# Splitting the epilogue's layer norm in two: statistics of a tile issued ahead of the next tile's preparation

## The chip, the cores and the metric

The kernel runs on the 8 cores of one Trainium2 chip (two dies of four cores). Each core computes 2048 of the 16384 rows. The metric is the device time of the slowest core in microseconds; lower is better.

## What is computed

A "sandwich" layer on x of 16384 x 1024, in fp32 at its borders. The reference, cut to its core:

```python
def _L0_attn_ref(x, Wq, bq, Wk, bk, Wv, bv):
    q = einsum('bte,de->btd', x, Wq) + bq
    k = einsum('bte,de->btd', x, Wk) + bk
    v = einsum('bte,de->btd', x, Wv) + bv
    p = softmax(einsum('bqd,bkd->bqk', q, k) / 32)
    return einsum('bqk,bkd->bqd', p, v)

def _L0_ffn_ref(x, W1, b1, W2, b2):      # BitNet: ternary weights, 8-bit activations
    h = gelu(bitlinear(x, W1, b1))
    return bitlinear(h, W2, b2)

x = x + _layernorm(_L0_attn_ref(_layernorm(x), ...))
x = x + _layernorm(_L0_ffn_ref(_layernorm(x), ...))
```

## The kernel before, in words

The whole program is written down through a small planner (`Plan`). `pl.op` and `pl.group` append instructions to one list for each engine, in the order in which the Python code calls them, and put waits in front of an instruction for the buffers that it reads and writes. Nothing reorders anything later: the order of calls is the order on each engine. A buffer is tracked as a whole (`bt(name)`), so the second of two transfers into the same buffer waits for the first.

There are four stages.

1. Layer norm of all 16384 rows into a DRAM scratch, quantising of the two FFN weights into DRAM scratches, and the q projection (0 to about 985 us in the profile).
2. Attention: 16 groups of 1024 keys by 4 groups of 512 queries, unnormalised z summed in `z_acc` in SBUF (to about 2976 us). Then the row sums' reciprocals go through DRAM into `linv_col` (to about 3040 us).
3. The epilogue of attention, which the change touches: 16 tiles of 128 rows, numbered t.
4. The FFN, again 16 tiles, after its weights have been loaded (3260 us to the end).

For a tile t the epilogue has three helpers, all with double buffers chosen by t % 2 but for the single `ep_znbf`:

- `ep_zn(t)`: VectorE scales `z_acc` by `linv_col` into `ep_znbf` (L817, called "zn" below); TensorE transposes it in 8 pieces into `ps_tz` (L825); VectorE copies the result to `ep_znfm` (L832, "the copy").
- `ep_proj(t)`: TensorE multiplies `ep_znfm` by `wv_ep`, 16 matmuls of 512 columns (L844) and 2 for the bias (L850), into `ps_pj`. I call these 18 matmuls the burst of tile t.
- `ep_out(t)`: the layer norm of `ps_pj` by `emit_ln` (two `bn_stats` L539 and L542, `bn_aggr` L545, plus-epsilon L548, all VectorE; the square root L551 on ScalarE; reciprocal L554 and the shift L557 on VectorE), then VectorE scales `ps_pj` into `x2_stage` (L868) and adds the residual `xr_tile` (L873). ScalarE issues the load of the residual two tiles ahead (L808), GpSimd issues the store of `x2_stage` (L880).

The loop (L885 to L894) calls `ep_zn(0)`, `ep_proj(0)`, and then for each t: `ep_zn(t+1)`, `ep_proj(t+1)`, `ep_out(t)`. So VectorE's list in one round is zn(t+1), copy(t+1), the whole of out(t). When the last projection, tile 15, has been emitted, the counts of all semaphores are kept in `gate_pj`.

After the epilogue SyncE's queue loads the FFN weights. The 32 transfers into `w2q_sb` (L906) are in order, each waiting for the one before. Transfers 0 to 15 wait only for the end of attention; transfer 16 waits for `gate_pj`, since its place in SBUF overlaps `wv_ep`. Behind the 16 last ones stand 8 transfers into `w1q_sb` (L916) and then the first loads of `x2_tile` (L935), which the FFN's first instruction (`emit_ln` in `stage_x(0)`) reads.

Of the kernel before, what the change touches and what calls it, by code (L numbers as in the profile page):

```python
# [10 lines left out]
AF = mybir.ActivationFunctionType  # L11
ALU = mybir.AluOpType
# [20 lines left out]
EPS = 1e-5  # L33
# [132 lines left out]
def build_program():  # L166
# [28 lines left out]
    pl = Plan()  # L195
    B = {}

    def bt(name):
        if name not in B:
            B[name] = BufT()  # L200
        return B[name]

    with ExitStack() as ctx:
# [64 lines left out]
        ln_scr2 = [at(f"ln_scr2_{i}", [P, 16], F32) for i in range(2)]  # L268
# [33 lines left out]
        def ms(ap_, val):  # L302
# [4 lines left out]
            out=ident[:], in_=ident[:], compare_op=ALU.not_equal, fill=1.0,  # L307
            base=0, pattern=[[-1, P]], channel_multiplier=1),
            reads=[bt("ident")], writes=[bt("ident")])
# [7 lines left out]
        for ec in range(EC):  # L317
            pl.op("gpsimd", lambda eng, ec=ec: eng.dma_start(
                out=bq_col[:, ec:ec + 1],
                in_=bq_in[ec * P:(ec + 1) * P].rearrange("(p o) -> p o", o=1)),  # L320
                writes=[bt("bq_col")], dma="LD_G")
        pl.op("gpsimd", lambda eng: eng.dma_start(
            out=bv_bcast[0:1, :], in_=bv_in[:]),
            writes=[bt("bv_bcast")], dma="LD_G")
        for (src, dst, nm) in ((wkt, wkt_sb, "wkt_sb"),
                               (wqt, wqt_sb, "wqt_sb")):
            for ec in range(EC):
                pl.op("gpsimd", lambda eng, s=src, d=dst, ec=ec:
                      eng.dma_start(out=d[:, ec, :],
                                    in_=s[ec * P:(ec + 1) * P, :]),  # L330
                      writes=[bt(nm)], dma="LD_G")
# [7 lines left out]
        def m_name(e_):  # L339
            return f"k_stage{e_}" if e_ < 4 else f"v_stage{e_ - 4}"  # L340

        for half in range(2):
# [7 lines left out]
                reads=[bt("bq_col"), bt("wkt_sb")], writes=[bt("ps_k0")])  # L350
        pl.op("vector", lambda eng: eng.tensor_copy(
            out=bq_row[0:1, :], in_=ps_k[0][0:1, :]),
            reads=[bt("ps_k0")], writes=[bt("bq_row")])
        for ec in range(EC):
# [3 lines left out]
            for half in range(2):  # L358
                for sc in range(EC):
# [8 lines left out]
                     reads=[bt("wqt_sb"), bt("wkt_sb")], writes=[psb])  # L368
            pl.op("scalar", lambda eng, ec=ec, pp=pp: eng.copy(
                out=m_chunks[ec][:], in_=ps_k[pp][:]),  # L370
                reads=[psb], writes=[bt(m_name(ec))])
# [166 lines left out]
        def emit_ln(eng_scr, scr_b, src_ap, src_b):  # L538
            pl.op("vector", lambda eng: eng.bn_stats(  # L539
                out=eng_scr[:, 0:6], in_=src_ap[:, 0:512]),  # L540
                reads=[src_b], writes=[scr_b])
            pl.op("vector", lambda eng: eng.bn_stats(  # L542
                out=eng_scr[:, 6:12], in_=src_ap[:, 512:1024]),
                reads=[src_b], writes=[scr_b])
            pl.op("vector", lambda eng: eng.bn_aggr(  # L545
                out=eng_scr[:, 12:14], in_=eng_scr[:, 0:12]),
                reads=[scr_b], writes=[scr_b])
            pl.op("vector", lambda eng: eng.tensor_scalar_add(  # L548
                out=eng_scr[:, 14:15], in0=eng_scr[:, 13:14], scalar1=EPS),
                reads=[scr_b], writes=[scr_b])  # L550
            pl.op("scalar", lambda eng: eng.activation(  # L551
                out=eng_scr[:, 14:15], in_=eng_scr[:, 14:15], func=AF.Sqrt),
                reads=[scr_b], writes=[scr_b])
            pl.op("vector", lambda eng: eng.reciprocal(  # L554
                out=eng_scr[:, 14:15], in_=eng_scr[:, 14:15]),
                reads=[scr_b], writes=[scr_b])
            pl.op("vector", lambda eng: eng.scalar_tensor_tensor(  # L557
                out=eng_scr[:, 15:16], in0=eng_scr[:, 12:13], scalar=-1.0,
                in1=eng_scr[:, 14:15], op0=ALU.mult, op1=ALU.mult),
                reads=[scr_b], writes=[scr_b])  # L560
# [65 lines left out]
        for g in range(NT_OWN // 4):  # L626
            xp = g % 4
            xfm = bt(f"xn_fm{xp}")
            for dc in range(DC):
# [7 lines left out]
                    for e_ in range(EC)]  # L637
# [6 lines left out]
                         reads=[bt(m_name(e_)) for e_ in range(EC)] +  # L644
                               [xfm, bt("bq_row"), bt("ones_row5")],
                         writes=[psb])
                pl.op("scalar", lambda eng, dc=dc, g=g:
                      eng.copy(  # L648
                          out=q_fm[:, dc, g * 512:(g + 1) * 512],
                          in_=ps_k[0][:, 0:512]),  # L650
                      reads=[psb], writes=[bt("q_fm")])
# [38 lines left out]
        for kg in range(NKG):  # L690
            par = kg % 2
            kb, vb = bt(f"k_buf{par}"), bt(f"v_buf{par}")
            if kg == NKG - 1:
                wv_gate = list(dict(pl.cnt).items())
                for ec in range(EC):
                    pl.op("gpsimd", lambda eng, ec=ec: eng.dma_start(
                        out=wv_ep[:, ec, :], in_=wvt[ec * P:(ec + 1) * P, :]),
                        writes=[bt("wv_ep")], dma="LD_G", extra=wv_gate)
            for qg in range(NQG):
                for kt in range(KT_PG):  # L700
# [9 lines left out]
                        reads=[kb, bt("q_fm")], writes=[pss])  # L710
                    pl.op("scalar", lambda eng, kt=kt, sp=sp: eng.activation(  # L711
                        out=p_sb[:, kt, :], in_=ps_s[sp][:], func=AF.Exp,
                        scale=1.0 / 32.0, bias=c_nshift[:]),
                        reads=[pss, bt("c_nshift")], writes=[bt("p_sb")])
                for qt in range(4):
# [8 lines left out]
                        reads=[bt("p_sb"), vb], writes=[psz])  # L724
# [5 lines left out]
                    reads=[bt("p_sb"), bt("ones_col")], writes=[bt("ps_l")])  # L730
                for qt in range(4):
                    psz = bt(f"ps_z{qt}")
                    t_own = qg * 4 + qt
                    if kg == 0:
                        pl.op("vector", lambda eng, qt=qt, t=t_own:
                              eng.tensor_copy(out=z_acc[:, t, 0:512],
                                              in_=ps_z[qt][:]),
                              reads=[psz], writes=[bt(f"z_acc{t_own}")])
                    else:
                        pl.op("vector", lambda eng, qt=qt, t=t_own:  # L740
                              eng.tensor_add(out=z_acc[:, t, 0:512],  # L741
                                             in0=ps_z[qt][:],
                                             in1=z_acc[:, t, 0:512]),
                              reads=[psz, bt(f"z_acc{t_own}")],
                              writes=[bt(f"z_acc{t_own}")])
                if kg == 0:
                    pl.op("vector", lambda eng, qg=qg: eng.tensor_copy(
                        out=l_acc[0:1, qg * QG:(qg + 1) * QG], in_=ps_l[:]),
                        reads=[bt("ps_l")], writes=[bt(f"l_acc{qg}")])
                else:  # L750
                    pl.op("vector", lambda eng, qg=qg: eng.tensor_add(
                        out=l_acc[0:1, qg * QG:(qg + 1) * QG], in0=ps_l[:],
                        in1=l_acc[0:1, qg * QG:(qg + 1) * QG]),
                        reads=[bt("ps_l"), bt(f"l_acc{qg}")],
                        writes=[bt(f"l_acc{qg}")])
                for qt in range(4):
# [9 lines left out]
                        reads=[bt("p_sb"), vb], writes=[psz])  # L766
                for qt in range(4):
                    psz = bt(f"ps_z{qt}")
                    t_own = qg * 4 + qt
                    if kg == 0:  # L770
                        pl.op("vector", lambda eng, qt=qt, t=t_own:
                              eng.tensor_copy(out=z_acc[:, t, 512:1024],
                                              in_=ps_z[qt][:]),
                              reads=[psz], writes=[bt(f"z_acc{t_own}")])
                    else:
                        pl.op("vector", lambda eng, qt=qt, t=t_own:
                              eng.tensor_add(out=z_acc[:, t, 512:1024],  # L777
                                             in0=ps_z[qt][:],
                                             in1=z_acc[:, t, 512:1024]),
                              reads=[psz, bt(f"z_acc{t_own}")],  # L780
                              writes=[bt(f"z_acc{t_own}")])
            if kg + 2 < NKG:
# [6 lines left out]
              reads=la, writes=la)  # L789
        pl.op("gpsimd", lambda eng: eng.dma_start(  # L790
            out=l_scr.rearrange("(o q) -> o q", o=1), in_=l_acc[0:1, :]),
            reads=la, writes=[bt("l_scr")], dma="LD_G")
        for tt in range(NT_OWN):
            pl.op("gpsimd", lambda eng, tt=tt: eng.dma_start(
                out=linv_col[:, tt:tt + 1], in_=l_scr[tt * P:(tt + 1) * P]),
                reads=[bt("l_scr")], writes=[bt("linv_col")], dma="LD_G")
# [5 lines left out]
        ps_pj = [ps2e.enter_context(nc.psum_tensor(f"ps_pj{i}", [P, E], F32))  # L802
                 for i in range(2)]
# [34 lines left out]
        def ep_proj(t):  # L838
            par = t % 2
            builds = []  # L840
            for half in range(2):
                for e_ in range(EC):
# [15 lines left out]
                     writes=[bt(f"ps_pj{par}")],  # L858
                     extra=(att_gateE if t < 2 else ()))

        def ep_out(t):
            par = t % 2
            ls = ln_scr2[t % 2]
            lsb = bt(f"ln_scr2_{t % 2}")
            emit_ln(ls, lsb, ps_pj[par], bt(f"ps_pj{par}"))
            sp = t % 2
            pl.op("vector", lambda eng, ls=ls, sp=sp, par=par:
                  eng.tensor_scalar(  # L868
                      out=x2_stage[sp][:], in0=ps_pj[par][:],
                      scalar1=ls[:, 14:15], scalar2=ls[:, 15:16],  # L870
                      op0=ALU.mult, op1=ALU.add),
                  reads=[bt(f"ps_pj{par}"), lsb], writes=[bt(f"x2_stage{sp}")])
            pl.op("vector", lambda eng, par=par, sp=sp: eng.tensor_add(  # L873
                out=x2_stage[sp][:], in0=x2_stage[sp][:],
                in1=xr_tile[par][:]),
                reads=[bt(f"x2_stage{sp}"), bt(f"xr_tile{par}")],
                writes=[bt(f"x2_stage{sp}")])
            if t + 2 < NT_OWN:
                xr_load(t + 2)
            pl.op("gpsimd", lambda eng, t=t, sp=sp: eng.dma_start(  # L880
                out=x2_scr[t], in_=x2_stage[sp][:]),
                reads=[bt(f"x2_stage{sp}")], writes=[bt(f"x2_scr_t{t}")],
                dma="LD_G")
# [2 lines left out]
        ep_proj(0)  # L886
        gate_pj = [None]
        for t in range(NT_OWN):
            if t + 1 < NT_OWN:
                ep_zn(t + 1)  # L890
                ep_proj(t + 1)
                if t + 1 == NT_OWN - 1:
                    gate_pj[0] = dict(pl.cnt)
            ep_out(t)  # L894
# [9 lines left out]
        for i in range(HC):  # L904
            g2 = pj_done if 16 <= i < 24 else att_gate
            pl.op("sync", lambda eng, i=i: eng.dma_start(  # L906
                out=w2q_sb[:, i, :], in_=w2q_scr[i]),
                reads=[bt("w2q_scr")], writes=[bt("w2q_sb")], dma="LD_S",
                extra=g2)
        pl.op("gpsimd", lambda eng: eng.dma_start(out=b1_row[:], in_=b1_in[:]),  # L910
              writes=[bt("b1_row")], dma="LD_G", extra=att_gate)
        pl.op("gpsimd", lambda eng: eng.dma_start(out=b2_row[:], in_=b2_in[:]),
              writes=[bt("b2_row")], dma="LD_G", extra=att_gate)
        w1_gate = att_gate + [zn_gates[8]]
        for i in range(EC):
            pl.op("sync", lambda eng, i=i: eng.dma_start(  # L916
                out=w1q_sb[:, i, :], in_=w1q_scr[i]),
                reads=[bt("w1q_scr")], writes=[bt("w1q_sb")], dma="LD_S",
# [14 lines left out]
        def x2_load(t):  # L933
# [7 lines left out]
              writes=[bt("thr_col")])  # L941
        pl.op("gpsimd", lambda eng: eng.memset(thr_col[:, 1:2], -6.25),
              writes=[bt("thr_col")])
# [286 lines left out]
```

How the kernel before makes its waits and increments, by code:

```python
    def _wait(self, engine, deps):  # L80
        wm = self.wm[engine]
        for sem, c in deps.items():
            if c <= 0 or wm.get(sem, 0) >= c:
                continue
            wm[sem] = c
            self.ops[engine].append(
                lambda eng, sems, s=sem, c=c: eng.wait_ge(sems[s], c))
# [8 lines left out]
    def op(self, engine, build, reads=(), writes=(), dma=None, extra=()):  # L96
        deps = self._deps(reads, writes, extra)
        if dma is not None:
            r = DMA_POOL[dma]
            sem = f"{dma}{self.rr[dma] % r}"
            self.rr[dma] += 1
            _merge(deps, sem, self.cnt[sem])
            inc = 16
        else:
            sem = ESEM[engine]
            inc = 1
        self._wait(engine, deps)
        self.cnt[sem] += inc
        n = self.cnt[sem]
        self.ops[engine].append(
            lambda eng, sems, build=build, s=sem, i=inc:
            build(eng).then_inc(sems[s], i))
        self._record(reads, writes, sem, n)
        return (sem, n)
# [1 line left out]
    def group(self, engine, builds, reads=(), writes=(), extra=()):  # L116
# [4 lines left out]
            self.ops[engine].append(  # L121
                lambda eng, sems, build=build, s=sem:
                build(eng).then_inc(sems[s], 1))
        n = self.cnt[sem]
# [12 lines left out]
            @block.sync  # L137
            def _(eng):
                for fn in self.ops["sync"]:
                    fn(eng, sems)
                for (s, c) in final:
                    if c > 0:
                        eng.wait_ge(sems[s], c)
```

## Time and profile before

| what | us |
|---|---|
| median of 3 runs | 4876.54 (4868.11 to 5015.16) |
| the profiled execution, its own time | 4887.02 |
| its span (slowest core, core 2) | 4885.5 |
| spans of the 8 cores | 4847.4 to 4885.5 |
| epilogue, first zn to the end of the last burst, core 2 | 3040.81 to 3172.01 |
| weight loads after it, until the FFN's first instruction | 3172.01 to 3259.92 |

All times are in microseconds from the start of the span, of the slowest core, unless a sentence says otherwise. PE is TensorE, DVE is VectorE, ACT is ScalarE, POOL is GpSimd, SPq the queue of SyncE. In a timeline row the figures are start, duration and what was done, and in square brackets how long the engine had been idle before and what released it. The ends of matmuls are modelled, and consecutive ones overlap by some tenths of a microsecond. The granted clock of TensorE (PEclk) is 1.00 at 2.4 GHz and 0.5 at 1.2 GHz; a value between is a stretch that had both.

### The profile page before, as it was taken

To read this page: it belongs to the slowest core of one execution; us is meant where nothing else is said; L and a number is where in the kernel's file an instruction comes from. 1 tells how busy PE (TensorE), PEld (TensorE's weight loads), DVE (VectorE), ACT (ScalarE), POOL (GpSimd) and SP (SyncE) were. 2 spreads that over 40 slices of the span, in tenths; PEclk is the share of its full clock that TensorE was granted. 3 is DMA by queue.
4 is the path that set the end of the run, shared out by engine and by line. 5 is a ranking of instruction groups with operands and counts; after the bars stand their busy time and mean duration, and the time that the engine had idled before them with its cause. 6 is when DMAs were issued, how large, how long until landed. Compare 5 with 4: busy or idle time off the path is not lost.

```text
span 4885.5 us, 38850 instructions; the slowest of 8 cores (4847.4 to 4885.5 us)
## 1 busy us (share of the span) xinstructions
PE 2908.4 (60%) x12406; PEld 1207.5 (25%) x12406; DVE 2049.9 (42%) x2949; ACT 785.7 (16%) x1131; POOL 83.9 (2%) x162
## 2 busy tenths in 40 slices
PE   2000003599999999999999994614444534454344
PEld 1000000134444444444444441201111111111111
DVE  0788786112221211121211222716665566655665
ACT  0000000111111111111111110002222222222221
POOL 1000001000000000000000000000000000000000
PEclk8555555789999999999999997856677767677677
DMA  4898765211111111111111111330000000000000
GB/s 86 254 276 271 229 239 183 69 46 35 35 35 35 35 35 35 35 35 35 35 35 35 35 18 43 124 117 9 9 9 11 15 9 9 9 18 9 9 9 9
DMA packets 245575, 315.07 MB, mean 64 GB/s; under 512 B 164448, under 2 KB 164480, under 8 KB 241280
## 3 DMA queue, kind: packets, MB, share of 16 engines
q10 hardware_dynamic: 47232, 134.24, 8.8%
q1 hardware_dynamic: 179072, 96.50, 8.3%
q0 software_dynamic: 19072, 81.83, 5.8%
q8 instruction: 106, 1.74, 0.2%
q14 instruction: 93, 0.76, 0.1%
HBM read 213.95 MB, written 67.12 MB: 58 GB/s over the span
## 4 chain that ended last, share of the span: by engine, by line
PE 49%; DVE 30%; DMA 9%; issue 7%; ACT 4%; DVEq 1%; ACTq 0%; SPq 0%; POOL 0%; POOLq 0%
PE ps_s L705 18%; PE ps_z L719 9%; PE ps_z L761 9%; PE ps_h L1044 4%; PE ps_l L726 2%; DVE f1k L973 2%; DVE f1k L976 2%; DVE f1k L952 2%; DVE f1k L965 2%; DVE f1k L969 2%; PE ps_o L1113 2%; ACT f1k L956 2%; DVE ln_scr L572 2%; DVE ln_scr L569 2%; DVE hs_col L1064 1%
## 5 line engine op out<-in xcount | busy, mean ns | idle before, releaser
L705 PE MATMUL ps_s<-q_fm,k_buf 128*128 128x512 bf16 x4096 | 911.3, 384 | 27.7 <-DMA k_buf<-xn_scr 27.7
L741 DVE TENSOR_TENSOR z_acc<-ps_z,z_acc 128x512 f32<-128x512 f32 x240 | 166.0, 692 | 1153.1 <-PE ps_z L719 1151.7
L711 ACT ACTIVATE p_sb<-ps_s,c_nshift 128x512 bf16<-128x512 f32 x512 | 351.8, 687 | 1631.6 <-PE ps_s L705 1631.6
L705 PEld LDWEIGHTS ps_s<-q_fm,k_buf 128*128 128x128 bf16 x4096 | 404.6, 99 | 523.8 <-issue 77.3
L719 PE MATMUL ps_z<-v_buf,p_sb 128*128 128x512 bf16 x2048 | 458.3, 382 | 72.6 <-ACT p_sb L711 70.8
L761 PE MATMUL ps_z<-v_buf,p_sb 128*128 128x512 bf16 x2048 | 459.1, 383 | 0.0
L1113 PE MATMUL ps_o<-w2q_sb,hq_fm 128*128 128x512 bf16 x1024 | 359.5, 529 | 85.4 <-ACT hq_fm L1103 85.4
L1044 PE MATMUL ps_h<-w1q_sb,xq_fm 128*128 128x512 bf16 x1024 | 275.2, 417 | 66.6 <-ACT h_sb L1057 65.1
L1098 PE MATMUL ps_t<-ident,hq_bf 128*128 128x128 bf16 x512 | 52.8, 266 | 426.4 <-DVE hq_bf L1091 426.4
L719 PEld LDWEIGHTS ps_z<-v_buf,p_sb 128*128 128x128 bf16 x2048 | 196.9, 98 | 334.1 <-issue 121.4
L777 DVE TENSOR_TENSOR z_acc<-ps_z,z_acc 128x512 f32<-128x512 f32 x240 | 165.9, 691 | 259.7 <-PE ps_z L761 258.3
L420 PE MATMUL ps_k<-ones_f32col,asums 128*1 128x1 f32 x2 | 0.2, 164 | 460.4 <-DVE asums L415 460.4
L761 PEld LDWEIGHTS ps_z<-v_buf,p_sb 128*128 128x128 bf16 x2048 | 196.6, 98 | 259.1 <-issue 46.8
L1025 PE MATMUL ps_t<-ident,xq_bf 128*128 128x128 bf16 x128 | 16.2, 306 | 369.1 <-DVE xq_bf L1014 369.1
L1113 PEld LDWEIGHTS ps_o<-w2q_sb,hq_fm 128*128 128x128 bf16 x1024 | 126.8, 128 | 300.9 <-issue 268.9
L633 PE MATMUL ps_k<-xn_fm,k_stage 128*128 128x512 bf16 x128 | 47.0, 506 | 253.6 <-ACT q_fm L648 253.0
L1098 PEld LDWEIGHTS ps_t<-ident,hq_bf 128*128 128x128 bf16 x512 | 40.3, 119 | 452.5 <-issue 452.5
L1044 PEld LDWEIGHTS ps_h<-w1q_sb,xq_fm 128*128 128x128 bf16 x1024 | 96.6, 104 | 212.2 <-issue 136.8
L1103 ACT COPY hq_fm<-ps_t 128x1024 bf16<-128x1024 bf16 x64 | 64.8, 1012 | 458.7 <-PE ps_t L1098 458.7
L956 ACT ACTIVATE f1k<-f1k 128x1024 f32<-128x1024 f32 x80 | 84.5, 1056 | 260.6 <-DVE f1k L952 260.6
L581 ACT ACTIVATE ln_scr<-ln_scr 128x1 f32<-128x1 f32 x128 | 25.9, 203 | 603.4 <-DVE ln_scr L578 600.0
L569 DVE BATCH_NORM_STATS2 ln_scr<-x_tile 128x6 f32<-128x512 f32 x128 | 87.8, 686 | 83.9 <-DMA x_tile<-x_in 83.8
(133 smaller groups left out, 2518.4 us busy)
## 6 DMA issues: line engine op xcount, KB each, us to landing
x_tile<-x_in ACTq DMA_DIRECT2D x128, 512.0 KB, 4.9
wq_stream<-w1t POOLq DMA_DIRECT2D x16, 2048.0 KB, 11.9
xn_scr<-xn_tm ACTq DMA_DIRECT2D x128, 256.0 KB, 5.1
wq_stream<-w2t POOLq DMA_DIRECT2D x64, 512.0 KB, 4.7
v_buf<-xn_scr SPq DMA_DIRECT2D x128, 256.0 KB, 2.6
w1q_scr<-wq_out ACTq DMA_DIRECT2D x8, 1024.0 KB, 11.3
w2q_scr<-wq_out ACTq DMA_DIRECT2D x32, 256.0 KB, 3.2
xr_tile<-x_in ACTq DMA_DIRECT2D x16, 512.0 KB, 4.1
```

Source lines behind the costliest of these rows:

```text
L569: pl.op("vector", lambda eng, ls=ls, t=t: eng.bn_stats(out=ls[:, 0:6], in_=x_tile[t % 4][:, 0:512]), reads=[xb], writes=[lsb])
L572: pl.op("vector", lambda eng, ls=ls, t=t: eng.bn_stats(out=ls[:, 6:12], in_=x_tile[t % 4][:, 512:1024]), reads=[xb], writes=[lsb])
L705: eng.matmul(ps_s[sp][:], k_buf[par][:, dc, kt * P:(kt + 1) * P], q_fm[:, dc, qg * QG:(qg + 1) * QG], start=(dc == 0), stop=(dc == DC - 1)))
L711: pl.op("scalar", lambda eng, kt=kt, sp=sp: eng.activation(out=p_sb[:, kt, :], in_=ps_s[sp][:], func=AF.Exp, scale=1.0 / 32.0, bias=c_nshi ...
L719: eng.matmul(ps_z[qt][:], p_sb[:, kt, qt * P:(qt + 1) * P], v_buf[par][:, kt, 0:512], start=(kt == 0), stop=(kt == KT_PG - 1)))
L726: (lambda eng, kt=kt: eng.matmul(ps_l[:], ones_col[:], p_sb[:, kt, :], start=(kt == 0), stop=(kt == KT_PG - 1)))
L741: eng.tensor_add(out=z_acc[:, t, 0:512], in0=ps_z[qt][:], in1=z_acc[:, t, 0:512]),
L761: eng.matmul(ps_z[qt][:], p_sb[:, kt, qt * P:(qt + 1) * P], v_buf[par][:, kt, 512:1024], start=(kt == 0), stop=(kt == KT_PG - 1)))
L777: eng.tensor_add(out=z_acc[:, t, 512:1024], in0=ps_z[qt][:], in1=z_acc[:, t, 512:1024]),
L956: pl.op("scalar", lambda eng: eng.activation(out=sq_ap, in_=d_ap, func=AF.Square), reads=[db], writes=[qb])
L1044: (lambda eng, e_=e_, hg=hg, hp=hp: eng.matmul(ps_h[hp][:], xq_fm[:, e_, :], w1q_sb[:, e_, hg * 512:(hg + 1) * 512], start=(e_ == 0), stop ...
L1113: eng.matmul(ps_o2[op_][:, half * 512:(half + 1) * 512], hq_fm[:, hc, :], w2q_sb[:, hc, half * 512:(half + 1) * 512], start=(hc == 0), sto ...
```

## The change

The layer norm of `ep_out` is cut behind the square root. A new helper `ep_stats(t)` has its first five instructions: the two `bn_stats`, `bn_aggr`, plus-epsilon, and the square root on ScalarE. `ep_out(t)` keeps the reciprocal, the shift, the scaling and the residual add. The loop calls `ep_stats(t)` first in each round, ahead of `ep_zn(t+1)`. No instruction is added or removed.

```diff
+        def ep_stats(t):
+            par = t % 2
+            ls = ln_scr2[t % 2]
+            lsb = bt(f"ln_scr2_{t % 2}")
+            src_b = bt(f"ps_pj{par}")
+            pl.op("vector", lambda eng, ls=ls, par=par: eng.bn_stats(
+                out=ls[:, 0:6], in_=ps_pj[par][:, 0:512]),
+                reads=[src_b], writes=[lsb])
+            pl.op("vector", lambda eng, ls=ls, par=par: eng.bn_stats(
+                out=ls[:, 6:12], in_=ps_pj[par][:, 512:1024]),
+                reads=[src_b], writes=[lsb])
+            pl.op("vector", lambda eng, ls=ls: eng.bn_aggr(
+                out=ls[:, 12:14], in_=ls[:, 0:12]),
+                reads=[lsb], writes=[lsb])
+            pl.op("vector", lambda eng, ls=ls: eng.tensor_scalar_add(
+                out=ls[:, 14:15], in0=ls[:, 13:14], scalar1=EPS),
+                reads=[lsb], writes=[lsb])
+            pl.op("scalar", lambda eng, ls=ls: eng.activation(
+                out=ls[:, 14:15], in_=ls[:, 14:15], func=AF.Sqrt),
+                reads=[lsb], writes=[lsb])
         def ep_out(t):
             par = t % 2
             ls = ln_scr2[t % 2]
             lsb = bt(f"ln_scr2_{t % 2}")
-            emit_ln(ls, lsb, ps_pj[par], bt(f"ps_pj{par}"))
+            pl.op("vector", lambda eng, ls=ls: eng.reciprocal(
+                out=ls[:, 14:15], in_=ls[:, 14:15]),
+                reads=[lsb], writes=[lsb])
+            pl.op("vector", lambda eng, ls=ls: eng.scalar_tensor_tensor(
+                out=ls[:, 15:16], in0=ls[:, 12:13], scalar=-1.0,
+                in1=ls[:, 14:15], op0=ALU.mult, op1=ALU.mult),
+                reads=[lsb], writes=[lsb])
...
         for t in range(NT_OWN):
+            ep_stats(t)
             if t + 1 < NT_OWN:
                 ep_zn(t + 1)
                 ep_proj(t + 1)
```

## Rows read from the trace of the kernel before

**Rows 1.** The page: the span, and TensorE's busy tenths in 40 slices.
```profile
span 4885.5 us, 38850 instructions; the slowest of 8 cores (4847.4 to 4885.5 us)
...
PE   2000003599999999999999994614444534454344
```

**Rows 2.** Stretches: epilogue, weight loads, FFN. Busy us by engine, PEclk, DMA share.
```profile
3040.81:3172.01 131.20, 91.64 (x416) 35.69 (x416) 89.03 (x152) 4.33 (x16) 7.46 (x14) 0.88 0.36 113
3172.01:3259.92 87.91, 0.00 (x0) 0.00 (x0) 5.67 (x9) 0.20 (x1) 2.25 (x6) 0.51 0.49 165
```

**Rows 3.** The chain that ended last, in one epilogue round: start, us, what.
```profile
3109.83 0.69 DVE ep_znfm L832
3110.52 0.62 DVE ln_scr L539
...
3116.24 0.67 DVE ep_znbf L817
```

**Rows 4.** Timeline of one clean epilogue round, both engines.
```profile
3109.11 0.61 PE L825 MATMUL ps_tz<-ident,ep_znbf 128*128 128x128 bf16 x8 [0.40 <-DVE ep_znbf L817]
3110.77 1.89 PE L844 MATMUL ps_pj<-wv_ep,ep_znfm 128*128 128x512 bf16 x8 [1.05 <-DVE ep_znfm L832]
3112.89 0.16 DVE L554 RECIPROCAL ln_scr<-ln_scr 128x1 f32<-128x1 f32 x1 [0.40 <-ACT ln_scr L551]
3114.74 0.39 PE L850 MATMUL ps_pj<-bv_bcast,ones_row_bf 1*128 1x512 bf16 x1
3116.16 0.75 DVE L817 TENSOR_SCALAR ep_znbf<-z_acc,linv_col 128x1024 bf16<-128x1024 f32 x1
3117.16 0.61 PE L825 MATMUL ps_tz<-ident,ep_znbf 128*128 128x128 bf16 x8 [2.03 <-DVE ep_znbf L817]
```

**Rows 5.** Timeline of TensorE at the end of burst 0 and at burst 1.
```profile
3050.78 0.39 PE L850 MATMUL ps_pj<-bv_bcast,ones_row_bf 1*128 1x512 bf16 x1
3051.10 0.62 PE L825 MATMUL ps_tz<-ident,ep_znbf 128*128 128x128 bf16 x8
3052.66 1.89 PE L844 MATMUL ps_pj<-wv_ep,ep_znfm 128*128 128x512 bf16 x8 [0.94 <-DVE ep_znfm L832]
```

**Rows 6.** Timeline from the last burst to the FFN's first instruction.
```profile
3171.62 0.39 PE L850 MATMUL ps_pj<-bv_bcast,ones_row_bf 1*128 1x512 bf16 x1
3172.94 39.36 SPq L906 DMA_DIRECT2D w2q_sb<-w2q_scr  x15
...
3259.92 0.69 DVE L539 BATCH_NORM_STATS2 ln_scr<-x_tile 128x6 f32<-128x512 f32 x1 [81.08 <-DMA x_tile<-x_scr]
```

**Rows 7.** Timeline of the FFN, where statistics directly follow a burst's last matmul.
```profile
3374.89 0.59 PE L1128 MATMUL ps_o<-b_row,ones_row_bf 1*128 1x512 bf16 x2
...
3375.58 0.70 DVE L1136 BATCH_NORM_STATS2 ln_scr<-ps_o 128x6 f32<-128x512 f32 x1 [7.87 <-PE ps_o L1128]
...
3377.50 0.15 DVE L1145 TENSOR_SCALAR ln_scr<-ln_scr 128x1 f32<-128x1 f32 x1
```

**Rows 8.** Timeline of TensorE in the epilogue: rounds with matmuls at the lower clock.
```profile
3060.54 0.61 PE L825 MATMUL ps_tz<-ident,ep_znbf 128*128 128x128 bf16 x8 [3.53 <-DVE ep_znbf L817]
3126.86 3.50 PE L844 MATMUL ps_pj<-wv_ep,ep_znfm 128*128 128x512 bf16 x8 [1.05 <-DVE ep_znfm L832]
...
3157.38 0.97 PE L825 MATMUL ps_tz<-ident,ep_znbf 128*128 128x128 bf16 x8 [2.03 <-DVE ep_znbf L817]
3159.40 3.57 PE L844 MATMUL ps_pj<-wv_ep,ep_znfm 128*128 128x512 bf16 x8 [1.05 <-DVE ep_znfm L832]
3162.91 0.60 PE L850 MATMUL ps_pj<-bv_bcast,ones_row_bf 1*128 1x512 bf16 x1
```

**Rows 9.** Timeline of TensorE in the FFN: the shortest of its 64 bursts.
```profile
4062.77 4.89 PE L1113 MATMUL ps_o<-w2q_sb,hq_fm 128*128 128x512 bf16 x16 [1.36 <-ACT hq_fm L1103]
```

**Rows 10.** Groups by line, FFN from 3260 us to the end, TensorE: busy us, mean ns.
```profile
L1113 PE MATMUL ps_o<-w2q_sb,hq_fm 128*128 128x512 bf16 x1024 | 359.5, 529 | 85.4 <-ACT hq_fm L1103 85.4
...
L1098 PE MATMUL ps_t<-ident,hq_bf 128*128 128x128 bf16 x512 | 52.8, 266 | 426.4 <-DVE hq_bf L1091 426.4
```

## The prediction

> **What bounds the kernel now.** I read the page first, for where the stage lies [rows 1]: the epilogue and the weight loads are slices 25 to 27 of 40. The stretches give their lengths [rows 2]: 131.2 us of epilogue, in which neither engine is full (TensorE 91.6 us busy, VectorE 89.0), and 87.9 us in which both are nearly idle. So the whole change plays in 2.7% of the span.
>
> Then I read the chain that ended last through one round [rows 3]. It runs from the copy straight into `bn_stats`, on through out(t), and comes to the next zn; TensorE is on it only for the eight transposes. The timeline of the same round [rows 4] shows the pitch: transposes start at 3109.11 and again at 3117.16, so 8.05 us a tile. TensorE's burst starts at 3110.77 and ends at 3114.74 + 0.39 = 3115.13, thus 4.36 us, and TensorE then idles 2.03 us until zn releases it. The burst of tile t+1 lies wholly beside VectorE's out(t), for out(t) reads the burst of tile t, which ended a round earlier. VectorE is the bound, and the burst is hidden with 2 us to spare. Over 14 rounds, from 3052.66 [rows 5] to the last burst's start at 3167.66, the mean pitch is 115.0 / 14 = 8.21.
>
> Last, does the stage's end set the kernel's end? The last burst ends at 3171.62 + 0.39 = 3172.01; the `w2q_sb` loads that waited for it resume at 3172.94, and the FFN starts at 3259.92 when `x2_tile` lands behind all of them [rows 6]. VectorE was idle 81 us before that. What delays the last burst delays the end one for one; what VectorE does after it (tiles 14 and 15) has 80 us of cover.
>
> **The change, step by step.** No work is added, only the order of VectorE's list moves. Before: zn(t+1), copy(t+1), stats(t), out(t). After: stats(t), zn(t+1), copy(t+1), out(t).
>
> *What it saves.* The square root's round trip, an idle of 0.40 us before the reciprocal [rows 4], now lies under zn, transposes and copy: at most 15 x 0.40 = 6.0 us, if VectorE stays the bound.
>
> *What it turns into a wait.* stats(t) reads burst t. In the new order it is the first thing in the round, so it is asked for right behind out(t-1), in the very period in which burst t runs. From copy(t), VectorE has only out(t-1) to do: reciprocal at 3112.89 to the end of the add at 3116.24 is 3.35 us [rows 3, 4], behind a copy of 0.69, so it is free some 4.05 us after the copy's start. The burst starts 3110.77 - 3109.83 = 0.94 after the copy's start and ends at 5.30. VectorE waits 1.3 us, and behind that wait stand zn(t+1) and copy(t+1), for which TensorE waits in turn. The ring closes: burst(t), stats(t), zn(t+1), transposes(t+1), copy(t+1), burst(t+1). Nothing in it overlaps. Its length:
>
> - burst at the higher clock: 4.36 [rows 4];
> - handover from the last matmul to `bn_stats`: 3374.89 + 0.59 = 3375.48 to 3375.58, 0.10 [rows 7];
> - stats: 3375.58 to 3377.50 + 0.15, 2.07 [rows 7];
> - zn's start to the transposes' start: 3116.16 to 3117.16, 1.00 [rows 4];
> - transposes' start to burst's start: 3109.11 to 3110.77, 1.66 [rows 4].
>
> The sum is 9.19 us, against 8.05: 1.14 more in each round, at an unchanged clock. ScalarE's root and out(t-1) are both inside the ring's shadow, and cost nothing (out has 1.3 us of slack).
>
> *The first round.* Before, zn(1) ran during burst 0 and its transposes followed the burst at once [rows 5]. Now stats(0) waits for burst 0 (3051.17), and burst 1 starts at 3051.17 + 0.10 + 2.07 + 1.00 + 1.66 = 3056.00 instead of 3052.66: 3.34 later. ScalarE's table load (1.28 us) is in this round, but only the reciprocal waits for it, later. Burst 15 then ends at 3056.00 + 14 x 9.19 + 4.36 = 3189.0 instead of 3172.0: **+17.0 us** with every burst at the higher clock.
>
> *TensorE's clock.* It is not at the higher level throughout: the granted clock of the stage is 0.88 [rows 2]. Going through its 15 rounds, in all 7 where TensorE had idled 0.8 us or less before the transposes the burst ran at 2.4 GHz; of the 8 with 2.03 to 3.53 us idle, 6 had part of the burst at 1.2 GHz [rows 8]. A typical such burst has 8 matmuls in 3.50 us instead of 1.89, so 1.6 us more; the one at 3159.40 cost more (3.57 - 1.89 here, more in its second half, 0.36 in the transposes). Before, a slow burst was mostly hidden under out(t). In the new ring it is on the path in full. And each new gap before the transposes is 0.10 + 2.07 + 1.00 = 3.17 us, on the side of the long ones. The nearest case is the FFN: 64 bursts of 16 matmuls behind eight transposes, with gaps of 2.8 to 4.5 us within a tile. Their busy time of 359.5 us is 5.6 each [rows 10], where 16 at the higher clock take about 3.6 (two groups of eight at 1.89 [rows 4], overlapping 0.17): 2.0 us lost, and the transposes lose 52.8 / 64 - 0.61 = 0.2 [rows 10]. The shortest of the 64 was 4.89 [rows 9], so each one had a slow part. I take a slow part in each of bursts 1 to 15, at the middle of 1.6 and 2.2: 1.9 us, 15 x 1.9 = 28.5. The bounds: none, 0; 6 of 8 instead of all, 21; everything at the lower clock, (3.57 - 1.89 + 0.60 - 0.39) twice plus 0.4 = 4.2 a round [rows 8], 63.
>
> The Trainium skill, "TensorE: Matmul & The Clock Gate", section "HAM oscillation — how this bites in real kernels", says that a loop of short bursts parted by long waits starts each burst throttled, and puts a kernel's loss at 26.7 us over 32 rounds. By that 0.83 a round, an estimate, the clock's part would be 12.5 us and the sum +29.5; this trace's slow bursts cost twice as much each, and they decide here.
>
> *The sum.* 17.0 + 28.5 = **+45.5 us**. On the profiled execution, 4887.0 + 45.5 = 4932.5. That execution is 10.5 us over the median of the runs, so for the median I expect 4876.5 + 45.5 = **4922 us**, 0.9% slower. Loads, x2 stores and residual loads keep their order; with a longer pitch they have more time. The FFN is not touched.
>
> **Rivals.**
>
> 1. *The clock mostly holds.* The ring closes, but bursts are slow only now and then. For it: two of eight long gaps went by without. Against: 64 of 64 in the FFN. Time: +17 to +35, 4894 to 4911.
> 2. *The clock stays down.* Idle is now near half of each round, and it might never rise for long. For it: bursts of 3.57 for eight matmuls exist. Against: no burst of the epilogue is slow to its end, nor was any of the FFN's. Time: +60 to +80, 4937 to 4957.
> 3. *Not slower: VectorE stays the bound.* If burst t were over before out(t-1) is, the moved statistics would wait for nothing, and only the root's 0.40 would show: pitch 7.65, 15 x 0.40 = 6 us faster, 4870. It decides at 4.05 - 0.94 - 0.10 = 3.0 us of burst; the shortest is 4.36, and only a modelled end that is over a microsecond too late could undo that. The FFN's handover of 0.10 speaks against it.
> 4. *The delay is swallowed behind the stage.* If the loads behind the gate waited for something else, the end would not move: 4877. The resumption 0.93 us after the last burst speaks against it [rows 6].
>
> **Chances.** The forecast with a slow part in nearly each burst (+35 to +60) 0.68; rival 1 0.17; rival 2 0.08; rivals 3 and 4 together 0.05, and 0.02 for what I don't see. For the range I reach from 4888 (into rival 1, with the low end of the runs before) to 4955 (rival 2). A comparison of this kernel tells some 2%, 97 us, from no change. All cases but the unseen lie within that: faster 0.01, within 2% 0.96, slower 0.03.
>
> **What would show it.** In the profile after: transposes wait about 3.2 us for zn in each round; `bn_stats` waits for TensorE's bias matmul (new, 1.3 us or more, 16 times); the reciprocal waits for nothing; the pitch is about 11 us, 9.2 where a burst is at 2.4 GHz; the stage's TensorE is on the chain that ended last; the last burst ends near 3217; the 88 us behind it are unchanged. A pitch below 8 makes the ring wrong, a pitch of 9.2 throughout makes the clock's part wrong, and a late FFN without a late gate makes the last step wrong.

## The result

The changed kernel is slower: the ratio of its time to that of the kernel before is 1.0084, with a 95% interval of 1.0053 to 1.0116. On 4873.5 us before, this is +41 us (26 to 57). In about half of the executions of either kernel one die ran at a lower clock for a time, so the ratio and all times below come from the others (4868.1 to 4876.5 us before; 4904.9 to 4910.2 after, with one at 4943.9), and the medians over all ten runs of each kernel, 4945.85 before and 4927.04 after, can't be compared.

The profiled execution of the changed kernel took 4906.95 us; its slowest core is core 7. Line numbers behind L861 have moved: the statistics in the epilogue are now L866 to L875, the root L878, the reciprocal L886, the residual add L900, and the weight loads L934 and L944.

First the stretches of the changed kernel, epilogue and weight loads, the counterpart of [rows 2]. The columns are the busy us of PE, PEld, DVE, ACT and POOL, then the granted clock, the DMA share and GB/s:

```profile
3020.63:3197.25 176.62, 111.07 (x416) 40.15 (x416) 90.09 (x152) 4.35 (x16) 7.99 (x15) 0.76 0.28 87
3197.25:3284.79 87.54, 0.00 (x1) 0.00 (x0) 4.65 (x8) 0.20 (x1) 1.72 (x5) 0.51 0.48 161
```

The epilogue grew from 131.2 to 176.6 us, the stretch behind it stayed at 88. VectorE's work is the same (90.1 us against 89.0), with as many instructions. TensorE issued the same 416 matmuls, but is busy for 111 us instead of 92, and its granted clock went from 0.88 to 0.76. The rise from 131.2 overstates the change a little: core 2, from which the 131.2 comes, had the shortest epilogue of the eight cores before, whose mean was 133.7; after, the mean is 176.5.

Now one round in the timeline, the counterpart of [rows 4]:

```profile
3078.57 0.61 PE L825 MATMUL ps_tz<-ident,ep_znbf 128*128 128x128 bf16 x8 [3.09 <-DVE ep_znbf L817]
...
3080.22 3.43 PE L844 MATMUL ps_pj<-wv_ep,ep_znfm 128*128 128x512 bf16 x8 [1.05 <-DVE ln_scr L886]
...
3082.00 1.23 DVE L900 TENSOR_TENSOR x_stage<-x_stage,xr_tile 128x1024 f32<-128x1024 f32 x1 [0.17 <-DVE x_stage L895]
...
3085.74 0.39 PE L850 MATMUL ps_pj<-bv_bcast,ones_row_bf 1*128 1x512 bf16 x1
3086.23 0.70 DVE L866 BATCH_NORM_STATS2 ln_scr<-ps_pj 128x6 f32<-128x512 f32 x1 [3.00 <-PE ps_pj L850]
...
3088.22 0.74 DVE L817 TENSOR_SCALAR ep_znbf<-z_acc,linv_col 128x1024 bf16<-128x1024 f32 x1
...
3089.22 0.61 PE L825 MATMUL ps_tz<-ident,ep_znbf 128*128 128x128 bf16 x8 [3.10 <-DVE ep_znbf L817]
```

Read it as a baton. VectorE ends the residual add of the tile before at 3083.23 and then stands still for 3.00 us, until the burst is over. The statistics take it to 3088.22, then zn; TensorE stands still for 3.10 us in that time. At no point is a burst beside statistics or zn. The same in the list of waits, us in total, times and longest:

```profile
DVE ln_scr L866 <- PE ps_pj L850: 56.6, 16, 6.3
...
PE ps_tz L825 <- DVE ep_znbf L817: 46.3, 15, 3.1
...
DVE ln_scr L886 <- ACT ln_scr L878: 0.4, 1, 0.4
```

The first wait did not exist before: there no statistics waited for TensorE. The last row is what the change did gain: the reciprocal's waits for the root have shrunk to one of 0.4 us, against 0.40 in each round [rows 4]. In the chain that ended last (start, us, what) the burst has come onto the path, where [rows 3] had only VectorE and the transposes:

```profile
3088.30 0.67 DVE ep_znbf L817
...
3089.22 0.62 PE ps_tz L825 x8
...
3090.88 3.23 PE ps_pj L844 x8
...
3096.68 0.71 DVE ln_scr L866
```

And behind the last burst, the counterpart of [rows 6]:

```profile
3196.87 0.38 PE L850 MATMUL ps_pj<-bv_bcast,ones_row_bf 1*128 1x512 bf16 x1
...
3198.19 41.88 SPq L934 DMA_DIRECT2D w2q_sb<-w2q_scr  x16
...
3284.79 0.69 DVE L539 BATCH_NORM_STATS2 ln_scr<-x_tile 128x6 f32<-128x512 f32 x1 [81.61 <-DMA x_tile<-x_scr]
```

The loads resume 0.94 us behind the last burst, as they did before (0.93).

### The profile page after: what moved, and what is told of

Read it like the earlier page. It is cut to its first block, busy times and chain, and to the rows that moved or that the text cites. A ratio compares the mean times of both kernels' runs of the same rounds, so it can differ in the third digit from the quotient of the medians.

```text
span 4905.4 us, 38864 instructions; the slowest of 8 cores (4889.1 to 4905.4 us)
## 1 busy us (share of the span) xinstructions
PE 2897.8 (59%) x12406; PEld 1205.7 (25%) x12406; DVE 2050.1 (42%) x2949; ACT 787.4 (16%) x1131; POOL 84.2 (2%) x162
## 4 chain that ended last, share of the span: by engine, by line
PE 49%; DVE 29%; DMA 9%; issue 7%; ACT 4%; DVEq 1%; ACTq 0%; SPq 0%; POOL 0%; POOLq 0%
PE ps_s L705 18%; PE ps_z L719 9%; PE ps_z L761 9%; PE ps_h L1072 4%; PE ps_l L726 2%; DVE f1k L1001 2%; DVE f1k L1004 2%; DVE f1k L993 2%; DVE f1k L980 2%; DVE f1k L997 2%; PE ps_pj L844 2%; PE ps_o L1141 2%; ACT f1k L984 2%; DVE ln_scr L572 2%; DVE ln_scr L569 2%
## 5 line engine op out<-in xcount | busy, mean ns | idle before, releaser
L705 PE MATMUL ps_s<-q_fm,k_buf 128*128 128x512 bf16 x4096 | 896.9, 380 | 28.6 <-DMA k_buf<-xn_scr 28.6
L719 PE MATMUL ps_z<-v_buf,p_sb 128*128 128x512 bf16 x2048 | 452.3, 379 | 74.6 <-ACT p_sb L711 70.8
L761 PE MATMUL ps_z<-v_buf,p_sb 128*128 128x512 bf16 x2048 | 453.1, 379 | 0.0
```

The source lines that it names most:

```text
L705: eng.matmul(ps_s[sp][:], k_buf[par][:, dc, kt * P:(kt + 1) * P], q_fm[:, dc, qg * QG:(qg + 1) * QG], start=(dc == 0), stop=(dc == DC - 1)))
L719: eng.matmul(ps_z[qt][:], p_sb[:, kt, qt * P:(qt + 1) * P], v_buf[par][:, kt, 0:512], start=(kt == 0), stop=(kt == KT_PG - 1)))
L761: eng.matmul(ps_z[qt][:], p_sb[:, kt, qt * P:(qt + 1) * P], v_buf[par][:, kt, 512:1024], start=(kt == 0), stop=(kt == KT_PG - 1)))
```

## The experiments

The theory on record has two terms: a serial ring of burst, statistics, zn, transposes and copy (17 us), and TensorE's clock, which falls in the gaps of that ring and makes part of each burst slow (28 us). The rivals: the slow bursts have another cause; early statistics cost something by themselves; the end of the epilogue doesn't set the end.

The table sums up what the timelines of all eight cores show. The epilogue is from the first zn to the end of the last burst; a burst that takes over 4.6 us is counted as slow, among bursts 1 to 15 of each core (burst 0 has a slow part in every kernel). The ratios are to the kernel before, with their 95% intervals; two of the kernels were not timed often enough for one.

| kernel | epilogue, 8 cores, us | mean | slow bursts of 15 | ratio of times |
|---|---|---|---|---|
| before | 131.2 to 135.3 | 133.7 | 6 or 7 | 1 |
| after | 175.6 to 176.8 | 176.5 | 15 | 1.0084 (1.0053 to 1.0116) |
| after_fill | 143.8 to 145.0 | 144.6 | 0 | 1.0017 (1.0006 to 1.0028) |
| after_fill4 | 164.0 to 166.4 | 165.4 | 15 | no interval |
| before_fill | 134.9 to 135.9 | 135.2 | 0 | no interval |
| zn_first | 130.8 to 157.2 | 142.6 | 5 to 13 | 1.0032 (1.0002 to 1.0062) |
| zn_first_fill | 121.4 to 122.5 | 121.8 | 0 | 0.9961 (0.9941 to 0.9981) |
| two_ahead | 111.6 to 117.0 | 113.6 | 3 to 6 | 0.9955 (0.9940 to 0.9971) |
| before_queue | 132.0 to 134.5 | 133.1 | 6 or 7 | 0.9836 (0.9809 to 0.9864) |
| two_ahead_queue_b | 113.3 to 117.1 | 114.9 | 3 to 6 | 0.9801 (0.9785 to 0.9816) |

### Filling TensorE's gap: which part is the clock?

```diff
# after_fill: behind each ep_proj(t), t < 15, of the changed kernel
# (ps_f, a PSUM tensor that nothing reads, is declared with the others)
+                pl.group("tensor", [
+                    (lambda eng, i=i: eng.matmul(
+                        ps_f[:], ident[:], wv_ep[:, 0, 0:512],
+                        start=(i == 0), stop=(i == 10)))
+                    for i in range(11)],
+                    reads=[bt("wv_ep"), bt("ident")], writes=[bt("ps_f")])
```

> The changed kernel with 11 matmuls of 512 columns added behind each burst but the last, into a PSUM bank that nothing reads; they fill about 2.4 of the 3.09 us in which TensorE waits for zn. Ring theory (17 us of the loss from the serial order, 28 us from TensorE's clock falling in each gap): with the gap filled the clock stays at 2.4 GHz, each burst takes 4.36 us instead of 6.25, the pitch is 9.1 us instead of 11.0, the epilogue is some 148 us long instead of 176.7, and the kernel about 28 us faster than the changed one and about 10 to 15 us slower than before. Rival (the slow part of a burst is there whatever TensorE does in the gap, or the fillers delay the transposes): bursts stay at 6.2 us, the epilogue at 177 us or more, the kernel 35 us or more slower than before.

Every burst from 1 to 15 on all eight cores took 4.1 to 4.4 us, the epilogue fell from 176.5 to 144.6, and the ratio from 1.0084 to 1.0017. The timeline of a round:

```profile
3105.04 0.39 PE L851 MATMUL ps_pj<-bv_bcast,ones_row_bf 1*128 1x512 bf16 x1
3105.36 2.55 PE L863 MATMUL ps_f<-wv_ep,ident 128*128 128x512 bf16 x11
3105.53 0.70 DVE L874 BATCH_NORM_STATS2 ln_scr<-ps_pj 128x6 f32<-128x512 f32 x1 [1.35 <-PE ps_pj L851]
...
3108.41 0.61 PE L826 MATMUL ps_tz<-ident,ep_znbf 128*128 128x128 bf16 x8 [0.50 <-DVE ep_znbf L818]
```

The ring is the same: statistics still wait for the burst, and these 1.35 us are the prediction's 1.3. But TensorE idles only 0.50 us before the transposes, and no matmul of bursts 1 to 15 runs at 1.2 GHz. In the stretch from 3060 to 3140 us the granted clock (third figure from the end) is 0.77 in the changed kernel, core 7, and 1.00 with the fillers, core 0:

```profile
3060.00:3140.00 80.00, 51.00 (x191) 18.40 (x190) 41.37 (x70) 1.43 (x7) 4.25 (x8) 0.77 0.31 93
```

```profile
3060.00:3140.00 80.00, 66.47 (x329) 27.43 (x333) 53.18 (x90) 1.82 (x9) 4.78 (x9) 1.00 0.40 119
```

So matmuls whose results nothing uses make the kernel 0.66% faster. Of the 42.9 us by which the epilogue grew on the mean of the cores, 31.9 go with the fillers and 11.0 stay. Not all of the 31.9 is the clock: with the fillers the transposes start 0.89 us behind zn's start instead of 1.00, and the burst 1.55 behind theirs instead of 1.66, so the pitch is 8.89 instead of 9.11, which is 14 x 0.22 = 3.1 us. The other 28.8 us are what the slow parts of bursts 1 to 15 and of their transposes add up to in the changed kernel, on the mean of the cores (27.6 of them in the bursts). The forecast for this run was some 148 us, and without the 3.1 it would be 147.7. Against the kernel before it is 8 us slower (3 to 14), a little under the 10 to 15 expected.

With 4 fillers instead of 11 (rows of core 0):

> The changed kernel with 4 instead of 11 unused matmuls behind each burst, 0.86 us of work, so TensorE's gap before the transposes goes from 3.09 to about 2.2 us, close to the 2.03 us that the kernel before had in its clean rounds. Theory (what matters is how long TensorE idles in a round): some bursts slow, some not, as in the kernel before, where 6 of the 8 rounds with a long gap were slow: 5 to 12 slow bursts of 15 on a core, epilogue between 155 and 170 us. Rival (any work in the gap, however short, keeps the clock up): no slow burst, 144 us as with 11.

```profile
3103.08 1.04 PE L863 MATMUL ps_f<-wv_ep,ident 128*128 128x512 bf16 x4
3106.13 0.61 PE L826 MATMUL ps_tz<-ident,ep_znbf 128*128 128x128 bf16 x8 [2.02 <-DVE ep_znbf L818]
3107.68 3.24 PE L845 MATMUL ps_pj<-wv_ep,ep_znfm 128*128 128x512 bf16 x8 [0.94 <-DVE ln_scr L894]
```

Here the expectation on the number of slow bursts was wrong: with a gap of 2.02 us, the same as in the clean rounds of before [rows 4], all 15 bursts on all cores had a slow part. It was smaller, 5.7 us a burst, and fell into a fixed rhythm, a pitch of 10.24. The epilogue is within the range given. The rival, that any filling is enough, fell with it. So the length of this gap alone does not tell whether a burst will be slow.

### The same fillers in the kernel before

> The kernel before with the same 11 matmuls of 512 columns behind each burst but the last. They take 2.4 us, more than the 2.03 us in which TensorE waited for zn in a clean round. Ring theory: in the old order slow bursts were mostly hidden under VectorE's work, so the clock's part is small: the epilogue goes from 131 to 135 us to 129 to 134 us, within a few us. Rival (the clock had cost the old order as much as the new one): 10 us or more shorter.

No burst from 1 to 15 was slow, and the epilogue was 134.9 to 135.9 us, not shorter than before. But this run can't decide between the theory and its rival. Eleven fillers (2.4 us) are longer than the 2.03 us of gap: they push the transposes back until TensorE has no gap at all before them (rows of core 4).

```profile
3105.51 2.55 PE L863 MATMUL ps_f<-wv_ep,ident 128*128 128x512 bf16 x11
...
3107.90 0.61 PE L826 MATMUL ps_tz<-ident,ep_znbf 128*128 128x128 bf16 x8
```

TensorE now sets a pitch of 8.22 us in most rounds (8.29 on the mean), longer than the 8.05 of a clean round before, so the epilogue could not have come out 10 us shorter whatever the clock had cost. The old timelines say it directly: bursts 1 to 15 lost 9.4 to 14.3 us to the lower clock, while 14 rounds took 114.4 to 116.3 us against 14 x 8.05 = 112.7. So 1.7 to 3.6 us of the loss showed, and the rest was under VectorE's work.

### Moving one call: who stands behind the wait?

```diff
# zn_first, against the changed kernel (ep_cp is the copy, cut out of ep_zn)
         for t in range(NT_OWN):
-            ep_stats(t)
             if t + 1 < NT_OWN:
                 ep_zn(t + 1)
+            ep_stats(t)
+            if t + 1 < NT_OWN:
+                ep_cp(t + 1)
                 ep_proj(t + 1)
...
```

> The changed kernel with one position moved: zn(t+1) is issued ahead of the statistics of tile t, the copy(t+1) stays behind them. The transposes can then follow the burst at once and VectorE's wait holds only the copy. Ring theory: the ring is burst 4.36 + handover 0.10 + statistics 2.0 + copy's start to the burst 0.94 = 7.4 us at the higher clock, and up to 9.3 with a slow part in each burst, against 9.1 and 11.0 in the changed kernel; so 20 to 25 us faster than the changed kernel, and between 10 us faster and 17 us slower than before. Rival (the loss comes from issuing the statistics early at all, whatever stands behind them): as slow as the changed kernel, 35 to 41 us over before.

It was 0.5% faster than the changed kernel and 0.3% slower than before, so the position of zn behind the wait costs, and early statistics alone do not cost as much as the rival had it. The ratio mixes this with the clock, because the cores part. All run the same instructions on the same shapes, yet four had epilogues of 131 to 135 us and four of 145 to 157. The stretch from 3060 to 3140 us, core 0 and core 1, with the granted clock again third from the end:

```profile
3060.00:3140.00 80.00, 54.22 (x261) 21.59 (x264) 58.04 (x99) 2.02 (x10) 4.88 (x10) 0.93 0.42 131
...
3060.00:3140.00 80.00, 59.85 (x206) 20.18 (x204) 46.30 (x81) 1.62 (x8) 4.25 (x8) 0.67 0.35 105
```

On core 0 a round with a burst at the higher clock takes 7.43 us, and 5 of 15 bursts are slow. On core 1 bursts 5 to 15 take 7.2 us each, nearly all of it at 1.2 GHz, at a pitch of 10.24; cores 3, 6 and 7 went the same way from burst 10, 5 and 7 on, and none of the four came out of it before the stage ended. Core 4 did: its bursts 3 and 4 took 7.18 and 7.00, and burst 5 was at 4.36 again. In the timeline of each, first core 0, then core 1:

```profile
3085.44 0.62 PE L825 MATMUL ps_tz<-ident,ep_znbf 128*128 128x128 bf16 x8
3088.58 1.89 PE L847 MATMUL ps_pj<-wv_ep,ep_znfm 128*128 128x512 bf16 x8 [2.52 <-DVE ln_scr L889]
```

```profile
3126.07 0.62 PE L825 MATMUL ps_tz<-ident,ep_znbf 128*128 128x128 bf16 x8
...
3129.20 3.57 PE L847 MATMUL ps_pj<-wv_ep,ep_znfm 128*128 128x512 bf16 x8 [2.52 <-DVE ln_scr L889]
```

The gap is the same 2.52 us on both. The kernel's time is that of the slowest core, so such a rhythm counts even if only one core falls into it.

Is it TensorE's gap that makes the rhythm? The same kernel with 11 fillers behind the transposes:

> zn_first with 11 unused matmuls behind each tile's transposes, in the 3 us in which TensorE waits for the copy. In zn_first three of eight cores had got stuck with bursts of 7.18 us and a pitch of 10.2, others had 5 slow bursts of 15 and a pitch of 8.0. Theory (the gap in TensorE's work lets its clock fall, and a slow burst does not by itself end that): all bursts 4.36 on all cores, pitch 7.4, epilogue about 123 us on each core, kernel some 15 us faster than zn_first and about 10 us faster than before. Rival (the order itself, or its position against the DMAs, makes the bursts slow): cores still differ, with epilogues of 131 to 157 us.

All 120 bursts were at 4.36, the cores agreed within 1.2 us, the pitch was 7.32, and the kernel was 0.39% faster than before. The order and its place against the transfers were the same as in zn_first, so the rival fell. (The expectation speaks of three cores with bursts of 7.18; the burst lists show four.) This run also settles what early statistics cost by themselves. Against after_fill, which has the same eleven fillers and no slow burst either, zn stands ahead of the statistics instead of behind them, and the epilogue is 121.8 us instead of 144.6. With early statistics it is even shorter than before (133.7).

### Two tiles ahead: opening the ring

```diff
# two_ahead, against the changed kernel
         ep_zn(0)
+        ep_cp(0)
         ep_proj(0)
+        ep_zn(1)
         for t in range(NT_OWN):
-            ep_stats(t)
             if t + 1 < NT_OWN:
-                ep_zn(t + 1)
+                ep_cp(t + 1)
                 ep_proj(t + 1)
...
+            ep_stats(t)
+            if t + 2 < NT_OWN:
+                ep_zn(t + 2)
             ep_out(t)
```

> zn and transposes are issued two tiles ahead. VectorE's list in a round is copy(t+1), statistics(t), zn(t+2), out(t), so the statistics read a burst that is a round old and zn covers the square root. Ring theory: no wait for a burst; VectorE's work sets the pitch, copy 0.61 + statistics 1.99 + zn 0.67 + out 3.28 = 6.55 us (TensorE's ring is 0.94 + 4.36 + 0.62 + 0.10 = 6.0); TensorE's gaps are short and its bursts mostly 4.36. Epilogue 108 to 112 us instead of 131 to 135, kernel 20 to 26 us faster than before, 0.5%. Rival (VectorE's pitch of 8 us was due to its own work and not to its waits): within 5 us of before.

The epilogue was 111.6 to 117.0 us, on most cores longer than the 108 to 112 expected, and the ratio 0.9955, which is 22 us (14 to 29). The timeline:

```profile
3106.22 0.69 DVE L835 COPY ep_znfm<-ps_tz 128x1024 bf16<-128x1024 bf16 x1 [1.01 <-PE ps_tz L825]
3106.83 0.69 DVE L869 BATCH_NORM_STATS2 ln_scr<-ps_pj 128x6 f32<-128x512 f32 x1
...
3108.81 0.74 DVE L817 TENSOR_SCALAR ep_znbf<-z_acc,linv_col 128x1024 bf16<-128x1024 f32 x1
...
3109.47 0.15 DVE L889 RECIPROCAL ln_scr<-ln_scr 128x1 f32<-128x1 f32 x1
```

Statistics and reciprocal wait for nothing in such a round: the first reads a burst that is a round old, the second has zn between itself and the root. Clean rounds take 6.49 us, VectorE's own work (forecast 6.55). The wait of 1.01 us at the copy follows a burst with a slow part; those were 3 to 6 of 15, and cost 1.1 us each here.

### Does the end of the epilogue set the kernel's end?

```diff
# before_queue: SyncE's queue in another order, all else as before
-        for i in range(HC):
-            (load of w2q_sb, i)
-        (loads of w1q_sb)
...
-        (x2_load(0), x2_load(1))
+        for i in list(range(16)) + list(range(24, 32)):
+            w2_load(i)
+        (loads of w1q_sb)
+        x2_load(0)
+        x2_load(1)
+        for i in range(16, 24):
+            w2_load(i)
```

> The kernel before with SyncE's queue in another order: the 24 w2q_sb loads that need only attention's end, then w1q_sb, then the first two x2_tile loads, and last the 8 w2q_sb loads that wait for burst 15. Nothing else is changed. Theory (the 88 us behind the epilogue are only transfers queued behind one gated transfer): they run under the epilogue, the FFN starts about 8 us after the last burst instead of 88, and the kernel is about 80 us faster than before, a ratio of 0.983 to 0.985. Rival (the transfers are bound by something that the epilogue uses too, or the FFN waits for the last w2q_sb): under 50 us.

The ratio was 0.9836: 80 us on the 4874 of before. The end of the last burst and the FFN's first instruction on core 2:

```profile
3151.83 0.39 PE L850 MATMUL ps_pj<-bv_bcast,ones_row_bf 1*128 1x512 bf16 x1
...
3164.41 0.69 DVE L539 BATCH_NORM_STATS2 ln_scr<-x_tile 128x6 f32<-128x512 f32 x1 [5.35 <-DMA x_scr<-x_stage]
```

12.2 us between them instead of 87.9 (9.7 to 14.2 over the cores, before 83.9 to 89.2). The expectation had 8. The 88 us were, for the most part, transfers that stood in line behind the gated ones (16 to 23) without needing the gate themselves. What ends the wait now is the store of the last x2 tile, which VectorE awaits before the FFN.

Both together, in two series; the first gave two times, 4776.65 and 4776.74 us, and no interval:

> two_ahead with the queue order of before_queue. Theory (what shortens the epilogue shortens the kernel one for one, with the transfers hidden too): 22 us + 80 us, about 102 us faster than before, ratio 0.979. Rival (with the transfers taken away from behind the stage, the transfers become the bound: 24 x 2.6 + 8 x 5 + 11 = 113 us from attention's end are not over when the shorter epilogue is): the gain of two_ahead is lost in part, no faster than before_queue.

> two_ahead_queue again, unchanged, for an interval: from its first runs a ratio of 0.979 to 0.981 is expected, against 0.9955 for two_ahead and 0.9836 for before_queue alone. If the gains don't add, 0.983 or more.

The ratio is 0.9801 (0.9785 to 0.9816), about 97 us. The two gains, 22 and 80 us, add up within their intervals. So what shortens the epilogue shortens the kernel by about as much, whether the loads follow it or run beside it. This is the fastest version of the study.

## Why the prediction was right, and where it was off

**The ring** was right in each link. From the round shown above: burst 3080.22 to 3086.13, handover 0.10, statistics to zn's start 1.99, zn to transposes 1.00, transposes to burst 1.66. Without the burst this is 4.75, where the prediction had 4.83; zn starts 0.08 before the end of the last small instruction. So the ring at the higher clock is 9.11, not 9.19. In the first round burst 1 started 4.54 us behind the end of burst 0, not 4.83 (4.9 on cores 2 and 4). That VectorE would wait 1.3 us for a burst of 4.36 shows as 1.35 in after_fill.

**The clock's term** was the largest and the least certain, and it was sized well. Forecast was a slow part in each of bursts 1 to 15, at 1.9 us. All 15 had one on all eight cores; the mean burst was 6.12 to 6.25 us, 1.76 to 1.89 over 4.36, and the transposes lost another 1.2 to 1.6 us in all. Together this is 28.8 us on the mean of the cores, where 28.5 was forecast. The FFN, not the epilogue's own past (6 of 8 on core 2, 52 of 66 on all cores), was the right neighbour for the count. That the slow part comes from TensorE's gaps, which was only argued, is shown by after_fill.

**The sum** is the step that failed, by its ring term and by its base. The forecast epilogue of 131.2 + 45.5 = 176.7 fits core 7 (176.6), but the difference was taken to the old epilogue of core 2, the slowest core of the profiled execution. That core was late because its attention ended late; its epilogue was the shortest of the eight. Against the mean of the cores the epilogue grew by 42.9 us, and with 28.8 for the clock the ring's term measures 14.0 us, not 17.0. In the changed kernel the spread has nearly gone (175.6 to 176.8), as each core is slow in each burst.

Nor did all of the 42.9 us reach the end. The mean span of the eight cores went from 4862.3 to 4897.4 us, by 35.1: what lies before the epilogue came out 5.2 us shorter, the stretch of the loads 0.8 and the FFN 1.9, parts that the prediction had left unchanged and whose code is unchanged. Whether that is chance or an effect is open. The ratio's +41 (26 to 57) covers both figures. So the forecast of 4922 us lies 12 to 17 us above all the times after the change but the one of 4943.9; all of them are inside the range of 4888 to 4955.

The base itself was thin. 4922 was meant as the median of the runs, on a median of three (4876.5), one of which was 5015.16. Over ten runs the same kernel has 4945.85 and the changed one 4927.04: these medians fell by 19 us where a rise of 45.5 was forecast, and the prediction had no term for such scatter.

**The rivals.** The clock mostly holds: not so, 15 of 15. Not slower, and delay swallowed: neither, by the waits and by before_queue. The clock stays down: not in this kernel. Its longest bursts are of 7.2 us, every fourth on core 7, and they too end at the higher clock, since their second eight matmuls take 2.83 us and not 3.57:

```profile
3101.32 3.57 PE L844 MATMUL ps_pj<-wv_ep,ep_znfm 128*128 128x512 bf16 x8 [1.05 <-DVE ln_scr L886]
...
3105.36 2.83 PE L844 MATMUL ps_pj<-wv_ep,ep_znfm 128*128 128x512 bf16 x8
```

Such bursts are no novelty. The prediction went through core 2 alone, where the longest of bursts 1 to 15 was 6.65; in the same execution of the kernel before, core 1 had one of 7.19:

```profile
3077.16 3.57 PE L844 MATMUL ps_pj<-wv_ep,ep_znfm 128*128 128x512 bf16 x8 [1.05 <-DVE ep_znfm L832]
...
3081.20 2.83 PE L844 MATMUL ps_pj<-wv_ep,ep_znfm 128*128 128x512 bf16 x8
```

zn_first came nearest to this rival: four cores there ended in bursts of 7.2 us, one after the other.

**The page of the Trainium skill** that the prediction weighed ("TensorE: Matmul & The Clock Gate", section "HAM oscillation — how this bites in real kernels") had it that short bursts parted by waits each start throttled; the count agrees, 15 of 15. Its loss of 0.83 us a round, an estimate from its figures, is under half of the 1.76 to 1.89 measured here.

**What the gain was.** The root's wait of 0.40 us a round is gone, as the change meant. It would have been 6 us. It was bought with the overlap of the burst with statistics and zn, which was worth more, and with TensorE's clock.

## What to carry to other kernels

When a result is consumed earlier in an in-order queue, look not at what the consumer costs but at what stands behind it: here the next tile's zn and copy waited with the statistics, and the engine that produced the result was itself waiting for them. Consume what is a whole round old, and issue what the other engine needs next ahead of anything that waits for it. And count a gap on TensorE twice as soon as the burst behind it is on the path: once as idle time, and once for the slower clock that the burst may then have (here in 52 of 66 bursts behind gaps of 2.0 us or more before, and in all 120 after).

## What the hardware showed that was not expected

- The same instruction stream held two rhythms on different cores of one chip: in zn_first rounds of mostly 7.43 us at a granted clock of 0.93, or of 10.24 us at 0.67, with the same 2.52 us gap of TensorE in both. The slow rhythm kept itself up although TensorE idled less in it (20 of 80 us, against 26). Why a core falls into one or the other stays open.
- The pitch of 10.24 us came up in two kernels, zn_first on its slow cores (bursts of 7.2) and after_fill4 on all (bursts of 5.7). Once a core had settled in that pitch, the granted clock fell and rose at the same places of every round, at a mean of 0.67 in zn_first (core 1) and 0.84 in after_fill4 (core 1, 3060 to 3140 us). No run tells whether the round keeps step with the clock or the clock with the round.
- A shortened gap need not help by halves: at 2.02 us before the transposes after_fill4 had 15 slow bursts of 15, where the kernel before, with 2.03 us in its clean rounds and 0.80 or less behind a slow burst, had 6 or 7.
- With the fillers TensorE took up its work 0.1 us sooner behind the instruction that released it (0.89 instead of 1.00 from zn to the transposes, and 1.55 instead of 1.66 from the transposes to the burst). The length of its idle does not explain it: after_fill4 has 0.89 behind 2.02 us of idle, and the kernel before has 1.00 behind 0.40 us as well as behind 2.03. The cause is open.
